# Mixing expert outputs with tokens on the partitions: a mixture-of-experts epilogue in a one-core block

## What is computed

```python
scores = _layernorm(agg, ln_gamma, ln_beta).reshape(M, HEADS, NUM_EXPERTS).mean(1)
topk_s, topk_i = jax.lax.top_k(scores, TOP_K)          # 2 of 4 experts
w = jax.nn.softmax(topk_s, axis=-1)
out = jnp.zeros_like(x)
for ei in range(NUM_EXPERTS):
    g = jnp.where(topk_i == ei, w, 0.0).sum(-1)         # one gate per token and expert
    hh = jax.nn.gelu(x @ W1[ei] + b1[ei], approximate=False)
    out = out + g[..., None] * (hh @ W2[ei] + b2[ei])
```

## Time and profile before

| | us |
|---|---|
| three runs, median (lowest to highest) | 8058.88 (8057.36 to 8060.34) |
| the profiled execution, its own time | 8058.64 |
| its span, first to last instruction | 8056.8 |

### The profile page before, as it was taken

How to read it: one execution, slowest core, us unless ns; L and a number is a source line. 1 busy time by engine, 2 the same in 40 slices (tenths; PEclk the granted TensorE clock), 3 DMA queues, 4 the chain that set the end, 5 groups by cost and what they waited for, 6 DMA issues and landing times.

```text
span 8056.8 us, 48889 instructions
## 1 busy us (share of the span) xinstructions
PE 3009.5 (37%) x14746; PEld 1474.1 (18%) x14746; DVE 3627.7 (45%) x3863; ACT 1934.5 (24%) x2929; POOL 4712.0 (58%) x4876
## 2 busy tenths in 40 slices
PE   3678887775122222222222212221212121200678
PEld 2345544442000100000001100000000000000222
DVE  5997788885323332333233324321211111111799
ACT  1446665552112121212121212121111111100000
POOL 1111121114777777777777777777777777776641
PEclk9889999897565666666666656665656565655555
DMA  1001111011122222222222222221111111111455
GB/s 52 26 26 34 34 34 34 29 32 57 45 70 57 70 65 62 57 70 69 58 57 70 71 56 57 70 54 31 41 31 41 31 41 31 39 18 46 137 184 173
DMA packets 284782, 455.39 MB, mean 57 GB/s; under 512 B 121214, under 2 KB 204382, under 8 KB 262366
## 3 DMA queue, kind: packets, MB, share of 16 engines
q1 hardware_dynamic: 134760, 395.08, 13.4%
q0 software_dynamic: 147648, 56.99, 6.4%
q10 hardware_dynamic: 2208, 1.05, 0.1%
HBM read 231.36 MB, written 221.42 MB: 56 GB/s over the span
## 4 chain that ended last, share of the span: by engine, by line
POOL 52%; issue 20%; DVE 3%; PE 1%; DMA 1%; POOLq 0%; ACT 0%; DVEq 0%
POOL gath L1319 51%; PE bank L1561 1%; DVE yo L1534 1%; POOL got L1596 1%; DMA gate_rows<-gate_dram 0%; DMA gate_dram<-turned_gates 0%; DVE fin L1539 0%; DVE s L1495 0%; DVE sc L1470 0%; POOL first L1749 0%; DVE s L1468 0%; DMA got<-edge_rows,end_i 0%; DVE sc L1482 0%; DVE sc L1489 0%; DVE sc L1474 0%
## 5 line engine op out<-in xcount | busy, mean ns | idle before, releaser
L1319 POOL DMA_INDIRECT gath<-node_rows,idx x4352 | 4125.3, 948 | 1326.3 <-issue 1326.3
L1272 PE MATMUL bank<-xm,w_s 128*128 128x512 f32 x1024 | 640.7, 770 | 3744.5 <-ACT scratch_i L1293 3732.3
L1228 DVE TENSOR_TENSOR adst_in<-bank,gath 128x256 f32<-128x256 f32 x68 | 53.4, 786 | 2819.5 <-DMA gath<-node_rows,idx 2819.5
L1272 PEld LDWEIGHTS bank<-xm,w_s 128*128 128x128 f32 x1024 | 227.4, 241 | 4142.8 <-ACT scratch_i L1293 3999.3
L1300 ACT ACTIVATE bank<-diff 128x256 f32<-128x256 f32 x68 | 26.3, 387 | 3740.4 <-DVE diff L1245 3740.4
L1046 POOL TENSOR_TENSOR scratch_i<-xc,dst_f 128x480 f32<-128x480 f32 x64 | 121.1, 1892 | 1128.6 <-ACT dst_f L956 1128.6
L1279 PE MATMUL bank<-scratch_i,w_s 128*128 128x512 f32 x1024 | 540.1, 685 | 195.7 <-ACT scratch_i L1293 118.5
L1215 DVE TENSOR_SCALAR scratch_i<-bank,b_s 128x512 f32<-128x512 f32 x256 | 190.4, 750 | 917.6 <-PE bank L1279 522.4
L1561 PE MATMUL bank<-gate_rows,choose 4*128 4x512 f32 x512 | 447.4, 1065 | 62.1 <-DVE yo L1534 50.5
L1293 ACT ACTIVATE scratch_i<-bank,b_s 128x512 f32<-128x512 f32 x512 | 345.1, 683 | 187.6 <-PE bank L1272 186.8
L1596 POOL DMA_INDIRECT got<-edge_rows,end_i x256 | 245.3, 958 | 208.3 <-DVE gates L1522 130.6
(11 more groups left out here) (216 smaller groups left out, 5650.0 us busy)
## 6 DMA issues: line engine op xcount, KB each, us to landing
gath<-node_rows,idx POOLq DMA_INDIRECT x4352
y_dram<-scratch_i SPq DMA_DIRECT2D x64, 1024.0 KB, 4.0
yo<-y_dram SPq DMA_DIRECT2D x64, 1024.0 KB, 5.1
edge_rows<-rows SPq DMA_DIRECT2D x68, 768.0 KB, 3.3
line<-moved SPq DMA_DIRECT2D x21, 2048.0 KB, 7.2
moved<-line SPq DMA_DIRECT2D x20, 2048.0 KB
scratch_i<-in_x SPq DMA_DIRECT2D x64, 256.0 KB, 2.7
x_dram<-x SPq DMA_DIRECT2D x64, 256.0 KB, 2.1
```

Source lines behind the costliest of these rows:

```text
L1272: e.matmul(bank[:, k % 2, :], w1_s[:, k // 2, P * (k % 2):P * (k % 2) + P], xm[par][:, :], start=True, stop=True).then_inc(up_full, 1)
L1319: e.indirect_dma_start(gath[par][:, j, :], None, node_rows, bass.IndirectOffsetOnAxis(ap=idx[par][:, j:j + 1].bitcast(U32), axis=0)).then_ ...
```

## The change

The expert outputs are kept with tokens on the partitions, `[token, expert, channel]`, in `y_dram` and in the buffers of the last stage. In the edge stage the second matrix product swaps its operands: 128 tokens of the hidden layer are the stationary operand, an expert's 128 x 128 matrix moves, and the 32 products of 128 columns for a chunk take the place of 8 of 512; b2 is a row spread over the partitions and is added with a tensor_tensor.

In the last stage a gate is then a scalar of its partition. For a quad (four blocks of 128 tokens) ScalarE multiplies experts 0 and 2 by their gates into PSUM (8 activations of 128 x 128, `first_terms`), VectorE multiplies experts 1 and 3 by theirs and adds ScalarE's terms (8 scalar_tensor_tensor of 128 x 128 into `mix`), PE turns the two halves of the mix back to channels on the partitions and adds them in PSUM (8 products of 128 columns with the identity as the moving operand), and VectorE adds `x1` (one tensor_tensor of 128 x 512) after it has mixed the next quad. The transposes, the copy, the way through DRAM, `choose` and the four products per quad go. The gates of a group are computed in one go at the group's start, not ahead during the group before.

```diff
     x1_dram = nc.dram_tensor("x1_dram", (C, M), F32, kind="Internal").ap()
     xn_dram = nc.dram_tensor("xn_dram", (C, M), F32, kind="Internal").ap()
     line = nc.dram_tensor("line", (MERGED + EDGES,), I32, kind="Internal").ap()
-    y_dram = nc.dram_tensor("y_dram", (M // 512, C, NE * 512), F32, kind="Internal").ap()
-    gate_dram = nc.dram_tensor("gate_dram", (2, P, P), F32, kind="Internal").ap()
+    y_dram = nc.dram_tensor("y_dram", (M // 512, P, 4 * NE * C), F32, kind="Internal").ap()
     with ExitStack() as ctx:
         scopes = [ctx]
...
             if experts:
-                for ex in range(NE):
-                    b = ex % 2
-                    e.wait_ge(y_full[b], c * 2 + ex // 2 + 1 + OPEN)
+                for n in range(4):
+                    b = n % 2
+                    e.wait_ge(y_full[b], c * 2 + n // 2 + 1 + OPEN)
                     e.wait_ge(y_saved, c - 1 + OPEN)
-                    e.tensor_scalar(yt[par][:, ex, :], bank[:, 2 + b, :], b2_s[:, ex:ex + 1], None,
-                                    ALU.add).then_inc(y_evac[b], 1)
+                    e.tensor_tensor(yt[par][:, n, :], bank[:, 2 + b, :], b2_row[:, :], ALU.add
+                                    ).then_inc(y_evac[b], 1)
...
-            for ex in range(NE):
-                b = ex % 2
-                e.wait_ge(y_evac[b], c * 2 + ex // 2 + OPEN)
-                for k in range(2):
-                    m = e.matmul(bank[:, 2 + b, :], w2_s[:, ex, k, :], hid[:, 2 * ex + k, :],
-                                 start=k == 0, stop=k == 1)
+            for n in range(4):
+                b = n % 2
+                e.wait_ge(y_evac[b], c * 2 + n // 2 + OPEN)
+                for ex in range(NE):
+                    for k in range(2):
+                        m = e.matmul(bank[:, 2 + b, C * ex:C * ex + C], hid[:, 2 * ex + k, P * n:P * n + P],
+                                     w2_s[:, ex, k, :], start=k == 0, stop=k == 1)
                 m.then_inc(y_full[b], 1)
...
-        def group_dve(e, g, par, i, more):
+        def terms_bank(b, h):
+            return bank[:, 2 * b + h, :].rearrange("p (n c) -> p n c", n=4)
+        def group_dve(e, g, par, i):
+            for part in range(3):
+                gates_dve(e, g, par, i + 1, part)
+            e.wait_ge(gates_ready, g + 1 + OPEN)
+            def mix_quad(k):
+                n = g * QUADS + k
+                e.wait_ge(first_terms, n + 1 + OPEN)
+                e.wait_ge(mix_turned, n - 1 + OPEN)
+                for h in range(2):
+                    for r in range(4):
+                        m = e.scalar_tensor_tensor(mix[k % 2][:, h, r], yo[k % DEEP][:, r, 2 * h + 1],
+                                                   gates[par][:, 4 * k + r, 2 * h + 1:2 * h + 2],
+                                                   terms_bank(k % 2, h)[:, r], ALU.mult, ALU.add)
+                m.then_inc(mixed, 1)
+            def finish_quad(k):
+                n = g * QUADS + k
+                e.wait_ge(mix_turned, n + 1 + OPEN)
+                e.wait_ge(fin_saved, n - DEEP + 1 + OPEN)
+                e.tensor_tensor(fin[k % DEEP][:, :], bank[:, 4 + k % 2, :], xo[k % DEEP][:, :],
+                                ALU.add).then_inc(fin_ready, 1)
             for k in range(QUADS):
-                b = k % DEEP
-                n = g * QUADS + k
-                e.wait_ge(spread, n + 1 + OPEN)
-                e.wait_ge(yo_loaded[b], g * (32 * QUADS // DEEP) + 32 * (k // DEEP + 1))
-                half = 4 * (k % 2)
-                e.tensor_tensor(yo[b][:, 0:NE, :], yo[b][:, 0:NE, :], bank[:, half:half + 4, :],
-                                ALU.mult).then_inc(weighed, 1)
-                e.wait_ge(weighed, n + 1 + OPEN)
-                e.wait_ge(fin_saved, n - DEEP + 1 + OPEN)
-                e.tensor_reduce(fin[b][:, :], yo[b][:, :, :].rearrange("c e t -> c t e"), AX,
-                                ALU.add).then_inc(fin_ready, 1)
-                if more and k in (1, 3, 5):
-                    gates_dve(e, g + 1, 1 - par, i + 1 + par, k // 2)
-        def turn_gates_pe(e, g, par):
-            e.wait_ge(gates_ready, g + 1 + OPEN)
-            e.transpose(bank[:, 4, 0:P], gates[par][:, :, :].rearrange("p n e -> p (n e)"), con("ident")
-                        ).then_inc(gates_turned, 1)
-        def group_pe(e, g, par, more):
+                e.wait_ge(yo_loaded[k % DEEP], g * (32 * QUADS // DEEP) + 32 * (k // DEEP + 1))
+                mix_quad(k)
+                if k:
+                    finish_quad(k - 1)
+            finish_quad(QUADS - 1)
+        def group_pe(e, g):
             for k in range(QUADS):
                 n = g * QUADS + k
-                e.wait_ge(weighed, n - 1 + OPEN)
-                if k == 0:
-                    e.wait_ge(rows_got, (g + 1) * 16)
-                if more and k == QUADS - 1:
-                    turn_gates_pe(e, g + 1, 1 - par)
-                    e.wait_ge(gates_copied, g + 2)
-                for ex in range(NE):
-                    m = e.matmul(bank[:, 4 * (k % 2) + ex, :], choose[:, ex, :],
-                                 gate_rows[par][:, 4 * k:4 * k + 4, :].rearrange("e b t -> e (b t)"),
-                                 start=True, stop=True)
-                m.then_inc(spread, 1)
+                e.wait_ge(mixed, n + 1 + OPEN)
+                e.wait_ge(fin_ready, n - 1 + OPEN)
+                for r in range(4):
+                    for h in range(2):
+                        m = e.matmul(bank[:, 4 + k % 2, P * r:P * r + P], mix[k % 2][:, h, r], con("ident"),
+                                     start=h == 0, stop=h == 1)
+                m.then_inc(mix_turned, 1)
...
-        def share_gates(e, g, par):
-            e.wait_ge(gates_turned, g + 1)
-            e.activation(turned_gates[:, :], bank[:, 4, 0:P], ACT.Copy).then_inc(gates_copied, 1)
-            e.wait_ge(gates_copied, g + 1)
-            e.dma_start(gate_dram[par], turned_gates[:, :]).then_inc(rows_put, 16)
-            e.wait_ge(rows_put, (g + 1) * 16)
-            e.dma_start(gate_rows[par][:, :, :], gate_dram[par].rearrange("(b e) t -> e b t", e=NE)
-                        ).then_inc(rows_got, 16)
         def group_act(e, g, par):
             for part in range(2):
-                gates_act(e, g + 1, part)
-            share_gates(e, g + 1, 1 - par)
+                gates_act(e, g, part)
+            e.wait_ge(gates_ready, g + 1 + OPEN)
+            for k in range(QUADS):
+                n = g * QUADS + k
+                e.wait_ge(yo_loaded[k % DEEP], g * (32 * QUADS // DEEP) + 32 * (k // DEEP + 1))
+                e.wait_ge(mixed, n - 1 + OPEN)
+                for h in range(2):
+                    for r in range(4):
+                        a = e.activation(terms_bank(k % 2, h)[:, r], yo[k % DEEP][:, r, 2 * h], ACT.Copy,
+                                         scale=gates[par][:, 4 * k + r, 2 * h:2 * h + 1])
+                a.then_inc(first_terms, 1)
...
-            e.tensor_copy(choose[:, :, :], con("ident")[0:NE, 0:NE].unsqueeze(2).broadcast_to([NE, NE, P]))
-            for part in range(3):
-                gates_dve(e, 0, 0, 1, part)
-            with e.Fori(0, GROUPS // 2 - 1) as i:
+            with e.Fori(0, GROUPS // 2) as i:
                 for par in range(2):
-                    group_dve(e, i * 2 + par, par, i, True)
-            for g in range(GROUPS - 2, GROUPS):
-                group_dve(e, g, g % 2, g // 2, g < GROUPS - 1)
+                    group_dve(e, i * 2 + par, par, i)
...
-                             *((b2_s[:, ex:ex + 1], b2[ex].unsqueeze(1)) for ex in range(NE))):
+                             (b2_row[:, :], b2.rearrange("e c -> (e c)").partition_broadcast(P))):
...
-                e.dma_start(yo[b][:, 0:NE, :], y_dram[bass.ds(t, 1)].rearrange("h c (e t) -> (h c) e t", e=NE)
-                            ).then_inc(yo_loaded[b], 16)
-                e.dma_start(yo[b][:, NE, :], x1_dram[:, bass.ds(t * 512, 512)]).then_inc(yo_loaded[b], 16)
+                e.dma_start(yo[b][:, :, :, :].rearrange("p n e c -> p (n e c)"),
+                            y_dram[bass.ds(t, 1)].rearrange("h p f -> (h p) f")).then_inc(yo_loaded[b], 16)
+                e.dma_start(xo[b][:, :], x1_dram[:, bass.ds(t * 512, 512)]).then_inc(yo_loaded[b], 16)
```

More of the change, by code:

```diff
@@ L280, in program @@
         yo_loaded = [sem(f"yo_loaded{b}") for b in range(DEEP)]
-        gates_turned = sem("gates_turned")
-        gates_copied = sem("gates_copied")
-        rows_put = sem("rows_put")
-        rows_got = sem("rows_got")
-        spread = sem("spread")
-        weighed = sem("weighed")
+        first_terms = sem("first_terms")
+        mixed = sem("mixed")
+        mix_turned = sem("mix_turned")
         fin_ready = sem("fin_ready")
@@ L363, in program @@
         b1_s = sb("b1_s", [P, NE, 2])
[L364 removed]
+        b2_row = sb("b2_row", [P, NE * C])
         xm = [sb(f"xm{b}", [C, 512]) for b in range(2)]
```

(35 more changed lines are left out.)

8 lines of the change are left out of this document (3 added, 5 removed).

## The result

| | us |
|---|---|
| the changed kernel, median of four runs (lowest to highest) | 7921.56 (7920.65 to 7924.63) |
| the kernel before, beside it | 8058.98 |
| ratio, 95% interval | 0.983 (0.9815 to 0.9846) |
| profiled execution: its time, its span | 7921.35, 7919.5 |

A forecast was written before the change was run, and what follows sets the result against it. Gathers bound the edge stage, VectorE the last stage; DMA would limit within groups after the change. Gates, hand-over, first passage, buffer return, three 4.02 us loads and last passage gave 50.9 us, times eight groups: 7882 us, range 7845 to 7955.

The forecast's parts named there:

- signs named for "right": Trace signs, mostly last stage: group 50 to 52 us, gates 15.4, quads 4 to 7 some 4 us apart, DMA near 0.9.
- small instructions: Rival, last stage: ScalarE and VectorE starts don't overlap, 0.37 and 0.34 us each; +21 us, 7903; chance 0.15.
- the slower rival: Last stage: PE loads each weight in the open at 1.2 GHz, 0.54 us per record, 8194 us; chance 0.03.
- no effect: Rival, last stage: exposed weight loads no longer than the product, 0.42 us per record, 74.3 per group, 8069; chance 0.02.
- First passage: Group's first quad, from ScalarE's terms through VectorE and PE to x1's addition: 8.65 us.
- hand-over: From the end of a group's gates to quad 0's first term on ScalarE: 0.05 us.
- last passage: Quad 7 of a group through the three engines: 6.95 us at 2.4 GHz or 8.65 at 1.2 GHz.
- the first buffer's return: Last stage: quad 0's buffer stored and reloaded with quad 4: 0.36 + 1.09 + 5.5 = 6.95 us.
- Quads 1 to 3 hide beside the returning loads: Last stage: quad 3 done 18.9 us after the gates, its buffer back at 25.8, DMA has quad 7 at 27.65 anyway.
- loads don't overlap: Rival, last stage: SP's landing waits make each buffer's return 6.95 us instead of 4.02; +70 us, 7952; chance 0.12.
- The clock: PE in the last stage: 1.2 GHz in a group's first quad, its last quad left between 1.2 and 2.4 GHz.
- the fast rival: Last stage: 2.4 GHz throughout and ScalarE starts at 0.20 us; 47.8 us per group, 7855; chance 0.06.

The follow-up runs named there:

- the seventh run: Changed kernel plus landing wait one quad later, x1 for quad 3 added before quad 4's mix, and 23 unread TensorE products per group during the gates: 7885.24 us.
- the late wait alone: Changed kernel, but SyncE waits for each store's landing one quad later, its 64 turns written out instead of looped: 7923.61 us, last stage 438.4.
- the early addition alone: Changed kernel, but from quad 4 of a group on VectorE adds x1 to the previous quad before each mix: 7980.95 us, ratio 0.9889.
- both returns (experiment 4): Changed kernel, but SyncE waits for landings one quad later and x1 for quad 3 is added ahead of quad 4's mix: 7899.88 us, last stage 425.6.

## Why the prediction was right, and where it missed

**The bound and the edge stage: right.** The gathers kept the edge stage; its end moved by 1.1 us. VectorE's work per quad fell as forecast, and the last stage gave all of the gain. Of the signs named for "right", two did not come: a group of 50 to 52 us (55.6), and quads 4 to 7 some 4 us apart (4.9).

**The engines' terms: right in kind, somewhat short.** ScalarE's activations are 0.294 us apart, not 0.27 (8 in 2.41 us against 2.25); VectorE's mix is 2.15 us, as forecast; x1's addition 0.69. PE's 16 records are 3.78 us at 1.2 GHz and 2.05 at 2.4, where the transposes and half-row products of the earlier trace rows had given 3.4 and 1.7. Starts do overlap, so "small instructions" was wrong. Weight loads lie beside the products (166.0 us of loads beside 178.5 of products), which removes the slower rival and "no effect": 0.236 us a record is far from 0.54 and 0.41. The rule in the Trainium skill, "TensorE: Matmul & The Clock Gate", "Part 3: Packing small matmuls — row/col tiling", that weight loads run beside products in flight only for other rows, does not hold for these full-row products; the same part of the Trainium skill also names a background weight buffer as a target of loads that are pulled ahead, which the prediction passed over. First passage, hand-over and last passage together missed by 0.77 + 0.14 + 0.69 = 1.6 us per group, 13 us in all; the first buffer's return missed by 0.45, 4 us in all.

**The step that failed: "Quads 1 to 3 hide beside the returning loads".** Its sentence put quad 3's buffer back at 25.8 us and the loads of quad 7 at 27.65 "anyway". In the trace quad 3's x1 ends 21.9 us after the gates, not 18.9, and quad 7's terms start 7631.90 - 7599.42 = 32.5 us after them. I had costed the return of one buffer and then let DMA's rate alone set the next three. But a return has two gates in program order: SyncE stands at the landing of the store before, and VectorE's x1 for quad 3 stands behind the mix of quad 4, which itself waits for a load. The change's text had both; I had costed the first only as a rival in which nothing overlaps (70 us) and named the second only for its cover on PE. Their price is 14.73 - 12.05 = 2.7 us per group, 21 us in all, and the run that takes both away shows 12.00 for that stretch. (Against the change beside it, the return there is 0.57 us longer and the last passage 0.58 shorter, so the group gains that 2.7 us in all; up to some 0.5 us of it may be the written-out turns.) The rate itself, 4.02 us a quad, was right.

**The rival "loads don't overlap"** was right in its mechanism (SyncE waits for landings) and wrong in its size: in the change a landing holds quad 2's store, and with it the loads of quad 6, until 2.6 to 4.8 us after the addition in every group, but the stores of quads 1 and 3 mostly go out after 0.4 us, so the loads still overlap. The measured time lies inside the range because the range reached up to this rival.

**The clock** was forecast low in a group's first quad, and was (16 records in 3.5 to 3.8 us, 2.05 at 2.4 GHz); the last passage, left between both levels, took 7.43 us in groups at 2.4 GHz and 9.16 at 1.2. What had not been asked is what its cure is worth. It takes 1.5 us off the first passage; of that 0.7 us a group was left alone, a size that is not sure, and 1.9 with the buffers back in time (52.87 to 51.00, of which the return gave 0.8).

That the forecast's total fits the seventh run is partly luck: that run has a shorter first passage than the forecast's and a longer return and load stretch. One sum is off by 3 us: the fast rival's 47.8 us per group make 7858, not 7855.

## What to carry to other kernels

When a buffer ring becomes the limit, write down for each buffer of the ring every instruction between its last use and its next load, on every queue in program order, and not for the first buffer alone; a wait for a landing in the issuing queue, or one addition behind a mix that waits for the same ring, delays the loads though the transfer rate is enough. Such delays can hide one another: the late wait alone gave 9 us of the 21 that both gave, and the early addition alone still had its store held for 4.3 to 6.6 us. And a DMA share of 0.94 does not say that DMA is full: look at the rate it has elsewhere.

## What was not expected of the hardware

The same 16 DMA engines, with the same transfers from quad 4's terms to quad 7's, were 0.88 to 0.98 busy at 318 to 351 GB/s in the change and 0.92 to 1.03 busy at 357 to 407 GB/s with both returns. A packet of 8 KB took 357 ns in the mean there and 330 here; why was not tried. A store of 256 KB landed 4.1 us after its issue in the changed kernel (median), with 1.3 MB of loads issued right behind it, and 5.8 us with both returns (experiment 4). TensorE's clock was still at 2.4 GHz behind a pause of 1.41 us and at 1.2 GHz for most of the work behind one of 4.58 us.
